# First stage of a two-layer kernel: 72-row mixing weights, the softmax ahead of the taps, the exchange behind tile 0

## The reference

```
# layer 0: a mixing over channels, chosen per sample by a small MLP with a softmax over K = 8
h   = gelu(gelu(cond @ W0 + b0) @ W1 + b1)
att = softmax(h @ W2 + b2)                         # (64, 8)
agg_w = einsum('bk,koi->boi', att, weight)         # one 64x64 matrix per sample
agg_b = att @ bias_k
y = einsum('boi,bih->boh', agg_w, x) + agg_b
x_q, sx = fp8_e4m3(y);  w_q, sw = fp8_e4m3(ffn_weight.T)   # one scale for a whole tensor: amax / 448
x = x + (x_q @ w_q) * (sx * sw) + bias
# layer 1
c = conv1d(x, conv_weight, 9 taps, 4 groups) + (cond @ c_weight.T)[:, :, None] + fside
x = x + c @ ((W_q - zero) * scale).T + bias        # 4-bit weight, a zero and a scale for 128 columns each
```

## Time and profile before

| | |
|---|---|
| median of three runs | 532.83 us (531.87 to 533.1) |
| profiled execution, its own time | 533.22 us |
| its span, first to last instruction | 531.3 us |
| PE busy | 509.3 us (96%) |
| DVE busy | 410.6 us (77%) |
| ACT busy | 245.5 us (46%) |
| POOL busy | 60.4 us (11%) |
| granted TensorE clock, mean | 0.994 |

### The profile page before, as it was taken

The page is one execution under the profiler, slowest core; times in us unless marked ns, Lnnn a source line. Parts: engine busy times, 40 slices in busy tenths (PEclk is TensorE's granted clock), DMA queues, the critical chain, the costliest instruction groups (busy, mean ns, idle before and its releaser), DMA issues.

```text
span 531.3 us, 9515 instructions
## 1 busy us (share of the span) xinstructions
PE 509.3 (96%) x3495; PEld 286.1 (54%) x3526; DVE 410.6 (77%) x519; ACT 245.5 (46%) x287; POOL 60.4 (11%) x67
## 2 busy tenths in 40 slices
PE   4999999879999999999999999999999999999997
PEld 3644444345555555555555555555555555555563
DVE  4789999885887777777777777777777777777652
ACT  3488897655344444444444444444444444442310
POOL 6257775011000000000000000000000000000000
PEclk9999999979999999999999999999999999999999
DMA  6999491144665566666666656566565656566632
GB/s 185 399 394 400 159 350 66 47 114 101 202 199 179 179 180 182 181 183 185 185 186 185 183 179 179 179 179 179 179 179 179 179 179 182 179 187 186 200 121 79
DMA packets 85387, 100.22 MB, mean 189 GB/s; under 512 B 34348, under 2 KB 66862, under 8 KB 85374
## 3 DMA queue, kind: packets, MB, share of 16 engines
q1 hardware_dynamic: 84554, 99.29, 59.4%
q0 software_dynamic: 448, 0.55, 0.6%
q10 hardware_dynamic: 372, 0.20, 0.1%
HBM read 58.41 MB, written 32.75 MB: 172 GB/s over the span
## 4 chain that ended last, share of the span: by engine, by line
PE 82%; DVE 11%; issue 2%; POOL 2%; ACT 1%; DMA 1%; SPq 0%; POOLq 0%; DVEq 0%; ACTq 0%
PE pair L1156 42%; PE pair L1130 19%; PE pair L1146 17%; DVE stat L802 5%; PE pair L1038 2%; PE pair L1120 1%; DVE work L729 1%; PE pair L1026 1%; DVE work L817 1%; DMA work<-work 1%; POOL work L454 1%; DVE Y L817 1%; DVE work L732 1%; POOL fixed L487 1%; POOL Y L467 1%
## 5 line engine op out<-in xcount | busy, mean ns | idle before, releaser
L1156 PE MATMUL pair<-f1T,work 128*128 128x512 f16 x1024 | 231.0, 379 | 0.0
L1156 PEld LDWEIGHTS pair<-f1T,work 128*128 128x128 f16 x1024 | 98.9, 98 | 113.5
L608 ACT ACTIVATE work<-Y,consts 128x1024 bf16 (+1 forms) x29 | 33.3, 1148 | 186.7 <-DVE work L891 186.7
L910 DVE TENSOR_TENSOR work<-Y,work 128x512 f16<-128x512 f16 (+1 forms) x64 | 71.2, 1118 | 46.6 <-ACT work L641 45.6
L1130 PE MATMUL pair<-f0T,work 128*128 128x512 bf16 x435 | 98.6, 379 | 1.5
L1146 PEld LDWEIGHTS pair<-taps,work 128*128 128x128 f16 x1536 | 90.7, 99 | 9.8 <-issue 2.4
L1146 PE MATMUL pair<-taps,work 128*128 128x128 f16 x1536 | 93.4, 222 | 2.3 <-DMA work<-work 2.3
L923 DVE TENSOR_TENSOR Y<-pair,Y 128x512 f32 (+1 forms) x64 | 43.9, 687 | 44.2 <-PE pair L1156 44.2
L641 ACT CAST work<-Y 128x512 f16 (+1 forms) x64 | 69.5, 1135 | 17.9 <-DVE Y L900 15.6
L1130 PEld LDWEIGHTS pair<-f0T,work 128*128 128x128 bf16 x464 | 45.4, 98 | 54.8
L1038 PE MATMUL pair<-Y,work 128*128 128x512 f32 x128 | 61.8, 618 | 1.1 <-ACT Y L581 0.7
(11 more groups left out here) (150 smaller groups left out, 234.8 us busy)
## 6 DMA issues: line engine op xcount, KB each, us to landing
Y<-in_x_dram SPq DMA_DIRECT2D x64, 512.0 KB, 3.9
out_dram<-Y SPq DMA_DIRECT2D x31, 512.0 KB, 3.8
split_rows<-work SPq DMA_DIRECT2D x30, 520.0 KB, 2.6
work<-split_rows SPq DMA_DIRECT2D x30, 520.0 KB, 3.9
Y<-in_L_ffn_weight_dram SPq DMA_DIRECT2D x8, 512.0 KB, 6.5
Y<-in_L_ffn_W_q_dram SPq DMA_DIRECT2D x5, 512.0 KB, 14.6
work<-in_L_ffn_W_q_dram SPq DMA_DIRECT2D x3, 512.0 KB, 15.2
work<-work SPq DMA_DIRECT2D x8, 65.0 KB, 3.6
```

Source lines behind the costliest of these rows:

```text
L910: nc.vector.tensor_tensor(split[:, r, s, 1], v[:, r, :], split[:, r, s, 0], ALU.subtract)\
L1156: last = mm(ps[2 + h][:, :], y1s[n][:, e, k, :], f1T[:, k, h * H:(h + 1) * H], start=False, stop=(e == 1 and k == KT - 1), skip_group_chec ...
```

## The change

It does the following, all in the first stage:

- The parts of the mixing weight stand in 72 rows: 3 parts of the softmax by 3 parts of the weight by 8 values of k. Row 9k + 3i + e holds part e of the weight for k, whatever i is. Each part is moved three times, and each of the nine transfers goes into eight partitions that are nine apart. SP issues six of them, POOL three. The 96 matmuls become 32 of 72 rows, and the three turned pieces of the softmax become one.
- SP issues the first three weight blocks at once, then its six transfers, and then the rest. POOL issues the two loads of the taps. The loads of `zs` come after the last weight block.
- DVE clears `mixw`: three of four parts at its start, the last behind the softmax. POOL doesn't any more, and arranges the taps behind its small memsets and its three transfers.
- DVE's sums of the taps move from ahead of the softmax to the exchange. TensorE turns the taps behind the mixing matrices.
- The exchange's two steps on TensorE move from tile 1 and behind it to behind tile 0 and into tile 1. DVE takes the largest value of tile 0 in round 0 of the loop and not ahead of the exchange's second half. DVE forms `wz` of block 0 itself; ACT's `scale_w0(0)` goes.
- TensorE turns `zs` behind tile 1 and not ahead of tile 0, and ACT copies them there.

```diff
-        KP = 3 * K
+        KP = 9 * K
...
@@ sync
-            for b in range(NB):
-                sp.dma_start(convraw[b * C:(b + 1) * C], convw).then_inc(ld["convw"], 16)
-            load_w0(0)
-            for e in range(3):
-                sp.wait_ge(wk_parts, (1, 3, 4)[e])
-                sp.dma_start(wkp3[e * K:(e + 1) * K, :], wkp[:, e, :]).then_inc(ld["wkp"], 16)
-                if e == 0:
-                    load_w0(1)
-            load_w0(2)
+            for r in range(3):
+                load_w0(r)
+            for e in range(2):
+                sp.wait_ge(wk_parts, (1, 3)[e])
+                for i in range(3):
+                    sp.dma_start(wkp9[3 * i + e:KP:9, :], wkp[:, e, :]).then_inc(ld["wkp"], 16)
+            load_w0(3)
+            load_w0(4)
             for b in range(NB):
                 sp.dma_start(mbk2[:, b * C:(b + 1) * C], cbk).then_inc(ld["mbk"], 16)
-            load_w0(3)
-            for z, src in enumerate((f1z, f1s)):
-                ...
-            load_w0(4)
             load_w0(5)
             load_mixing(0)
             load_w0(6)
             load_w0(7)
+            for z, src in enumerate((f1z, f1s)):
+                ...
@@ gpsimd
+            for b in range(NB):
+                pool.dma_start(convraw[b * C:(b + 1) * C], convw).then_inc(ld["convw"], 16)
             nc.gpsimd.memset(wide_taps, 0.0).then_inc(taps_zero, 1)
-            for n in range(4):
-                nc.gpsimd.memset(mixw[:, n * R8:(n + 1) * R8, :], 0.0).then_inc(mixw_zero, 1)
+            ... (the five small memsets)
+            pool.wait_ge(wk_parts, 4)
+            for i in range(3):
+                pool.dma_start(wkp9[3 * i + 2:KP:9, :], wkp[:, 2, :]).then_inc(ld["wkl"], 16)
@@ scalar
-            act.wait_ge(zs_mm, 1)
...
                 if t == 1:
+                    act.wait_ge(zs_mm, 1)
+                    nc.scalar.copy(zs, ps[6][:, 384:384 + P // 2].bitcast(fp16)).then_inc(zs_ev, 1)
+                if t == 2:
                     act.wait_ge(w_step, 2)
-                    scale_w0(0)
@@ vector
+            for n in range(3):
+                clear_mixw(n)
...
-            dve.wait_ge(ld["convw"], 32)
-            dve.wait_ge(tapcols_made, 3)
-            for part in (tapsum, tapsum2):
-                ...
             largest_w0(0)
...
+            clear_mixw(3)
...
-            largest_mixed(0)
+            dve.wait_ge(ld["convw"], 32)
+            ... (the two sums)
             dve.wait_ge(w_pe, 1)
...
             scales(w_inv, w_mul, ps[7][:, 128:129], w_step)
+            nc.vector.tensor_scalar(wz[0], w0f[:, 0, :], w_mul, None, ALU.mult).then_inc(w0v_first, 1)
...
                 less_w1(r)
+                if r == 0:
+                    largest_mixed(0)
@@ tensor
+            pe.wait_ge(ld["wkp"], 96)
+            pe.wait_ge(ld["wkl"], 48)
+            pe.wait_ge(attp_ev, 1)
             for q in range(4):
                 for j in range(8):
                     o2 = 8 * q + j
-                    for i in range(3):
-                        last = mm(ps[q][:, j * B:(j + 1) * B], wkp3[:, o2 * 2 * C:(o2 + 1) * 2 * C],
-                                  attpT[:, i], start=(i == 0), stop=(i == 2))
+                    last = mm(ps[q][:, j * B:(j + 1) * B], wkp9[:, o2 * 2 * C:(o2 + 1) * 2 * C],
+                              attpT, start=True, stop=True)
...
                     if t == 1 and h == 0:
-                        pe.wait_ge(w_red, R8 + 1)
-                        nc.tensor.transpose(ps[7][0:1, 0:P], w_part, ident[:, :]).then_inc(w_pe, 1)
+                        pe.wait_ge(w_red, R8 + 2)
+                        mm(ps[7][:, 128:129], ones, w_all, start=True, stop=True).then_inc(w_pe, 1)
...
                 mixed_tile(t)
+                if t == 0:
+                    pe.wait_ge(w_red, R8 + 1)
+                    nc.tensor.transpose(ps[7][0:1, 0:P], w_part, ident[:, :]).then_inc(w_pe, 1)
```

More of the change, by code:

```diff
@@ L244, in adaln_ffn_kernel @@
         w0v = sem("w0v")
+        w0v_first = sem("w0v_first")
         w0q = sem("w0q")
@@ L738, in _, with clear_mixw @@
         def _(dve):
+            def clear_mixw(n):
+                nc.vector.memset(mixw[:, n * R8:(n + 1) * R8, :], 0.0).then_inc(mixw_zero, 1)
+            for n in range(3):
+                clear_mixw(n)
             dve.wait_ge(ld["wk"], 16)
@@ L1076, in _ @@
                 mixed_tile(t)
+                if t == 0:
+                    pe.wait_ge(w_red, R8 + 1)
+                    nc.tensor.transpose(ps[7][0:1, 0:P], w_part, ident[:, :]).then_inc(w_pe, 1)
                 if t == 1:
-                    pe.wait_ge(w_red, R8 + 2)
-                    mm(ps[7][:, 128:129], ones, w_all, start=True, stop=True).then_inc(w_pe, 1)
+                    pe.wait_ge(ident_cast, 3)
+                    pe.wait_ge(agg_done, 2)
+                    pe.wait_ge(ld["zs"], 32)
+                    for z in range(2):
+                        for g in range(NG):
+                            o8 = (z * NG + g) * KT
+                            last = nc.tensor.transpose(ps[6][:, 384:384 + P // 2].bitcast(fp16)[:, o8:o8 + KT],
+                                                       zst[:, z, g::NG], ident_h[0:KT, 0:KT])
+                    last.then_inc(zs_mm, 1)
                 if t == 11:
```

76 lines of the change are left out of this document (33 added, 43 removed).

## The result

| | before | changed |
|---|---|---|
| median of 20 runs each, side by side | 533.34 us (531.87 to 535.33) | 531.07 us (528.02 to 533.97) |
| ratio, with its 95% interval | | 0.9952 (0.9941 to 0.9963) |
| profiled execution, its own time | 533.22 us | 531.02 us |
| its span | 531.3 us | 528.8 us |
| granted TensorE clock, mean | 0.994 | 0.994 |

The change makes the kernel 0.48% faster. The ratio times the first median of 532.83 is 530.3 us, against a forecast of 529.4 and a range of 526.8 to 533.6. The likeliest case came true with two thirds to three quarters of its size: 2.2 us between the profiled executions where 3.4 were forecast.

What follows compares the result with a forecast made beforehand. The prediction took the chain of waits before the loop, then DVE in the loop (61.35 of 63.84 us busy), as the bound. Terms -4.9 + 1.2 + 0.3 = -3.4 gave 529.8, and 0.4 lower for the median: 529.4 us; range 526.8 to 533.6.

Steps and rivals of the forecast that it cites:

- Softmax: Before the loop: without POOL's wait, exponential at about 8.6 us and parts at 10.2, 3.3 us sooner.
- Memsets: DVE's clearing of mixw: 0.7 us each, three hidden ahead of a load, the fourth on DVE's path, 10.2 to 10.9.
- Matrices: TensorE's 32 mixing matmuls: start at 11.6 us after the nine transfers, take 1.8, done at 13.4 against 19.73.
- DVE up to the exchange: DVE from 10.9 us: four weight blocks to 15.5, place_last to 16.9, three blocks to 20.4.
- Loads: Weight loads: transfers cost 0.1 us each of 0 to 0.6; block 7 lands at 19.7, last reduction ends 20.9.
- The exchange: Turn behind tile 0, spread after half of tile 1 at slow pace: scale ready at 24.0 us against 28.59, -4.6.
- The loop's start: DVE's own wz takes 0.96 us; first row at 25.0 against 29.87, -4.9; tile 0's 1.22 moves into round 0: -3.7.
- Round 0: Loop's first round: DVE's wait for tile 2 is 0 to 1.5 us, taken as 0.3.
- TensorE stays slow: Rival: TensorE slow through tiles 2 and 3, DVE waits 1.5 and 1.3 us more; -0.9, 531.9 us; chance 0.12.
- The nine transfers eat the loads: Rival: weight loads before block 7 lose 0.75 us for each transfer, block 7 at 25.6; 535.0 us; chance 0.15.
- Nothing moves: Rival: the loop follows something else than its start, above all the stream of x; 532.8 us; chance 0.05.
- POOL late: Rival: POOL's three transfers wait for DVE, matrices come at 17 us, not 13.4; -1.9, 530.9 us; chance 0.11.

Runs made afterwards that it cites:

- Experiment 8: Changed kernel with a lean start: SP issues block 3 between its transfer groups, POOL clears mixw's last quarter, POOL's taps wait for the softmax's parts; ratio 0.9961.
- late softmax: Changed kernel, but POOL clears mixw first, ahead of its transfers and taps, and DVE sums the taps ahead of weight block 0 and the softmax; ratio 1.0050.
- experiments 4 and 7: Changed kernel with the exchange as before, within and behind tile 1: 0.9971; changed kernel with the scale's spread first, ahead of tile 1: 0.9971.
- experiment 1: Changed kernel with each of the nine transfers going into eight neighbouring partitions, not eight that are nine apart; ratio to the kernel before 0.9998.
- softmax alone: Kernel before with only DVE's sums of the taps moved to the exchange and TensorE's turn of the taps behind the mixing matrices; ratio 0.9994.
- all nine on SP: Changed kernel with all nine transfers issued by SP and none by POOL; ratio to the kernel before 0.9953.
- 24 rows: Changed kernel with the 24-row weights of the kernel before: three transfers, three turned softmax pieces, 96 matmuls; ratio to the kernel before 0.9969.

## Why the prediction was right, step by step

The mechanism was right: a sooner loop is a sooner end of the stage, by 3.31 of 3.79 us. The 530.3 us lie in the stated range, and also in the narrower one that the forecast had by itself, 527.8 to 530.8 (its upper end is a slip: the slow tile 2 of the sum, -2.2, gives 530.6). The sizes of its steps:

1. *Softmax.* The exponential came as said, at 8.88 (said: 8.6), though block 0 landed at 7.28 and not at 6.3. The parts were there at 11.25 and not at 10.2. Four of the five small steps behind the reciprocal took 0.34 to 0.37 where they took 0.17 to 0.22, and the fifth 0.24 where it took 0.16: POOL's copies of the taps, moved to 9.06, run beside them.

```profile
9.06 2.78 POOL L475 COPY Y<-f0T 128x128 f32<-128x128 f32 x8
```

   I had costed the taps as a thing that TensorE wants late, and not as a neighbour of DVE. Experiment 8 takes the neighbour away, and the steps take 0.16 to 0.27. What is left above the kernel before (0.22 for a cast that took 0.17) goes with the new order of the parts; the late softmax has it too, with POOL idle.

2. *Memsets.* 0.91 each, and not 0.7. Three were not quite hidden: with 0.16 between them the third holds the first cast until 4.00, though its load has landed at 3.60. But since POOL's memsets no longer run beside it, the first cast took 0.35 where it took 1.13, and the split ends at 6.24, 0.34 sooner than before.

3. *Matrices.* From 13.27 to 15.16 (said: 11.6 to 13.4), with 1.52 us of waiting for a transfer. It cost nothing: DVE's copies began at 16.86 without a wait, since DVE was itself late: what was 15.5 in step 4 had become 16.83.

4. *DVE up to the exchange.* Its durations held; it started 1.3 late from steps 1 and 2.

5. *Loads.* This was the term that was mis-sized. Block 3 was issued at 8.87 as said and landed 5.4 later, at 14.3 and not at 12.5; block 7 at 21.03 and not at 19.7. On block 3 that is 1.8 more than without any cost, so 0.2 for each of nine transfers, within the range of 0 to 0.6, and not 0.1; in experiments 4 and 7, with the same loads, it is 0.3 (15.1 and 14.9). That it is all theirs is an inference: block 0, ahead of them, was late too, by 1.0.

6. *The exchange.* The last reduction ended at 22.27 (20.9), the scale was ready at 25.26 (24.0). The half tile at the slow pace took 1.87 (said: 1.8).

7. *The loop's start.* DVE's `wz` took 0.76 and not 0.96. The start was 26.08: −3.8, and not −4.9. The 1.1 that is missing is the 1.3 by which the scale was late, less these 0.2. Of the 1.3 DVE's own late start makes 1.0; the wait of 0.36 for block 7 is the rest. So with quicker small steps the loads would still have held it, as in the profile of experiment 8.

8. *Round 0.* No wait (said: 0.3). And a gain that I had not seen: round 1 took 6.58 us between its first row and that of round 2, against 7.21. L729 there takes 0.42 and not 0.91, because POOL's pass L483 now ends at 33.3 and no longer stands beside it; in the kernel before that pass (L481 there) ran from 35.17 to 37.08 and DVE's row was this:

```profile
36.46 0.91 DVE L729 TENSOR_SCALAR work<-work 128x1024 int16<-128x1024 int16 x1
```

So the stage gained 3.3 where the sum said 3.4, by errors that cancel: the start gained 1.1 less, and rounds 0 and 1 did better by 0.4 and 0.6. That agreement is luck. Between the stage and the total the prediction had set nothing: "a microsecond won before the loop is a microsecond at the end". In the pair of profiles 0.8 went in the second stage and 0.3 outside the span (531.02 less 528.8 is 2.2, before it was 1.9). But both lie in what executions of one kernel differ by: at the same clock of 0.994 the same code behind the stage took 438.5 to 439.7 us in four kernels, and 16 of the 20 executions of the changed kernel stand 1.8 or 1.9 above their spans, the other four 2.2 to 2.5. So these 1.1 us don't show the quoted sentence wrong.

What the ratio lacks is another question: 0.48% of 533.34 is 2.6 us, against the 3.4 of the sum and the 3.3 of this stage. One part may be the profile: it has the earliest block 7 of the three kernels with its loads. With 21.68 or 21.89 in place of 21.03, and the half tile as slow as here, the stage would gain 2.4 to 2.7 (an estimate; the kernel before, whose DVE didn't wait for its block 7 at 22.70, would not move). But in seven of the nine kernels of the table the stage says more for the kernel than its ratio does, by 0.2 to 1.6 us, so a little may be lost behind the stage after all, or the profile of the kernel before may stand late. What makes up this difference stays open. By the rows the one term clearly mis-sized is that of step 5, the loads.

Of the rivals, *TensorE stays slow* was half right: it stayed slow up to the half tile at 22.69, which the sum had priced and which is most of DVE's wait of 1.47, but not for tile 2, for which DVE didn't wait at all. *The nine transfers eat the loads* names the right resource, at 0.2 or 0.3 instead of 0.75; experiment 1, at 0.68, is that rival made true. *Nothing moves* is out: the stage's end moved with the loop's start. *POOL late* did not come: its three transfers were issued within 1.78 us from 6.55, and landed by 12.68, before SP's last at 13.22.

```profile
6.55 1.78 POOL L462 DMA_DIRECT2D Y<-work  x3 [2.85 <-DVE work L752]
```

The Trainium skill, "SBUF — State Buffer", SBUF: two separate sides, which spoke against this step by a lock on descriptors, is not contradicted by this: DVE was idle up to 7.30 and reducing then, and by the same page a reduction leaves POOL free. No run here issues the three beside a copy or a cast of DVE.

## What to carry to other kernels

When one small tensor has to be moved within the on-chip memory while a large stream of loads is running, look at which partitions it goes to before you count its bytes: the same nine transfers cost the stream 3 to 4 us more into eight neighbours than into eight that are nine apart. And when several waits stand in a row ahead of a loop, a part of a change can't be judged by itself: the softmax alone gave 0.5 us of the loop's start and nothing in the time. An experiment that takes a part back out can cost more than the part is worth, as the 5.4 us of the late softmax do, if it puts new work and old work on one list. Compare single profiles only for differences above what the same code shows between executions, here up to about 1 us in a landing. And an idle time in brackets, as the 1.47 us here, is a gain only if what it waits for can come sooner without making the next thing late.

## What the hardware showed that I had not expected

TensorE's pace. Up to some time in the exchange, its 128x512 products in float32 took 0.85 to 0.94 us, the pace of 1.2 GHz, though it had worked with short pauses since the mixing matrices; afterwards they took 0.43 to 0.56. The granted clock of 1.00 in the rows of the start, which the prediction set against the slow matmuls, is no record: in each trace the records of the clock begin only at the switch, and the view shows 1.00 for what lies ahead of them. They begin at 24.76 before the change and at 24.33 in the changed kernel. The matmuls of the kernel before that start up to 24.03 have the slow pace, those from 24.82 on the quick one; in the changed kernel the last slow one starts at 23.59 and the first quick one at 24.79. The others have 26.17 (neighbouring partitions), 23.32 (all nine on SP), 24.85 (24 rows), 29.39 (softmax late), 26.39 (softmax alone), 23.48 (spread first) and 24.32 (lean start). "Exchange as before" has 17.54, so that tile 0 was already quick at 19.16, and then 0.50 from 24.4 to 31.2. The pace before the switch shows only in the length of the matmuls. The half of tile 1 ahead of the spread so took 1.02 to 1.87 us, and in some kernels a late load cost less for that reason. What sets the time no run here shows.

POOL beside DVE slows even very small steps. In the new order of the parts a cast of 64 x 24 took 0.22 with POOL idle (all nine on SP, late softmax, lean start) and 0.31 to 0.36 beside POOL's copies (the changed kernel, exchange as before, spread first). In the old order, with neighbouring partitions, the casts took 0.17 beside the same copies, and the subtractions between and behind them grew instead, to 0.41 and 0.45 from 0.16 and 0.17. And a DVE pass over 128 x 1024 of 16 bits took 0.91 beside POOL's pass over two tensors and 0.42 without it.
